# Context projections as three bf16 products, a split completion signal for the stacked keys, and a new item order in two cross attentions

## The reference

```python
kh = (memory @ wk.T + bk).reshape(Bx, -1, H, d).transpose(0, 2, 1, 3)
vh = (memory @ wv.T + bv).reshape(Bx, -1, H, d).transpose(0, 2, 1, 3)
a = softmax(einsum('bhnd,bhmd->bhnm', qh, kh) / sqrt(d))
ca = einsum('bhnm,bhmd->bhnd', a, vh)
```

## Time and profile before

| | |
|---|---|
| median of 3 runs | 2066.61 us (2065.41 to 2078.53) |
| profiled execution, its own time | 2067.55 us |
| its span, first to last instruction | 2065.7 us |
| mean granted clock of TensorE | 0.95 of full speed |
| busy: PE, DVE, ACT, POOL | 1846.1, 1401.8, 1259.3, 325.4 us |
| XA0, main loop | about 89 to 590 us |
| XA1, main loop | about 1039 to 1765 us |

### The profile page before, as it was taken

How to read it: one execution, slowest core, us unless ns; L and a number is a source line. 1 busy time by engine, 2 the same in 40 slices (tenths; PEclk the granted TensorE clock), 3 DMA queues, 4 the chain that set the end, 5 groups by cost and what they waited for, 6 DMA issues and landing times. The chain is left out here.

```text
span 2065.7 us, 65669 instructions
## 1 busy us (share of the span) xinstructions
PE 1846.1 (89%) x28558; PEld 1189.3 (58%) x28576; DVE 1401.8 (68%) x2411; ACT 1259.3 (61%) x1785; POOL 325.4 (16%) x331
## 2 busy tenths in 40 slices
PE   8899999999989577999689999999999999757798
PEld 5577777777765364444355656656566665425443
DVE  3677777777753665566487888888888888238465
ACT  3477777777744371333267877777777877438343
POOL 4000000000030430111001100010001100014265
PEclk8999999999999787999799999999999999878999
DMA  4454555445400300555644455455555452030011
GB/s 146 103 142 126 130 133 136 128 125 131 112 10 1 62 4 16 148 146 144 121 87 98 83 93 92 84 97 88 93 88 94 85 93 40 1 63 4 22 41 42
DMA packets 66540, 178.18 MB, mean 86 GB/s; under 512 B 20276, under 2 KB 24500, under 8 KB 65844
## 3 DMA queue, kind: packets, MB, share of 16 engines
q1 hardware_dynamic: 64436, 170.85, 37.7%
q10 hardware_dynamic: 1824, 3.20, 0.7%
HBM read 84.39 MB, written 1.31 MB: 41 GB/s over the span
## 5 line engine op out<-in xcount | busy, mean ns | idle before, releaser
L604 ACT ACTIVATE Pb<-ps 128x1024 f32<-128x1024 f32 (+2 forms) x640 | 633.7, 1001 | 206.5 <-PE ps L553 158.8
L676 DVE TENSOR_REDUCE MX<-ps 128x2 f32<-128x804 f32 (+1 forms) x386 | 368.9, 986 | 59.8 <-PE ps L520 58.7
L573 PE MATMUL ps<-Pb,V 128*17 128x64 f32 (+1 forms) x13312 | 360.3, 248 | 9.7 <-issue 4.9
L678 DVE TENSOR_REDUCE MX<-ps 128x1 f32<-128x402 f32 (+1 forms) x512 | 278.1, 571 | 102.2 <-PE ps L524 92.9
L573 PEld LDWEIGHTS ps<-Pb,V 128*17 128x17 f32 (+1 forms) x13312 | 256.3, 97 | 97.0 <-issue 64.3
L520 PE MATMUL ps<-KST,QW 50*128 50x402 bf16 (+1 forms) x1024 | 176.6, 340 | 23.9 <-ACT V L623 17.1
L553 PE MATMUL ps<-QW,KST 50*128 50x128 bf16 (+1 forms) x3328 | 165.5, 219 | 29.9 <-ACT Pb L604 29.3
L504 PE MATMUL ps<-W,CT 128*128 128x128 f32 (+1 forms) x1144 | 168.3, 286 | 1.1 <-ACT V L623 1.1
L553 PEld LDWEIGHTS ps<-QW,KST 50*128 50x128 bf16 (+1 forms) x3328 | 101.1, 96 | 113.1 <-ACT Pb L604 83.9
L496 PE MATMUL ps<-CT,W 128*128 128x402 f32 (+1 forms) x352 | 146.8, 542 | 18.0 <-DMA CT<-ctxT 12.1
L524 PE MATMUL ps<-KST,QW 96*128 96x402 bf16 (+1 forms) x512 | 154.3, 339 | 4.3 <-issue 2.2
(11 more groups left out here) (235 smaller groups left out, 2764.8 us busy)
## 6 DMA issues: line engine op xcount, KB each, us to landing
CT<-ctxT SPq DMA_DIRECT2D x44, 800.5 KB, 4.8
KST<-HL SPq DMA_DIRECT2D x320, 100.1 KB, 3.0
KST<-C SPq DMA_DIRECT2D x320, 100.1 KB, 3.0
Pb<-routed SPq DMA_DIRECT2D x64, 256.0 KB, 3.9
ABO<-ctxT SPq DMA_DIRECT2D x10, 800.5 KB, 5.4
T<-ctxT SPq DMA_DIRECT2D x10, 800.5 KB, 4.4
KST<-HL SPq DMA_DIRECT2D x128, 50.0 KB, 2.7
KST<-C SPq DMA_DIRECT2D x128, 50.0 KB, 2.7
```

The source lines that it names most:

```text
L573: mm = nc.tensor.matmul(ps[32 * quad:32 * quad + m, SUM, oc:oc + nh * S], V[0:n, b % 2, tile, v0:v0 + m], Pb[0:n, buffer(b, x), ti * att.W ...
L604: nc.scalar.activation(Pb[0:n, buffer(b, x), 0:banks * 512].rearrange("p (a c) -> p a c", a=banks), score_banks(b, x)[0:n, 0:banks, :], AC ...
L676: nc.vector.reduce_max(MX[:, b % 2, 2 * j:2 * j + 2], work(job)[:, :, 0:n], AX.X).then_inc(freed["dve"], 1)
L678: nc.vector.reduce_max(MX[:, b % 2, j:j + 1], work(job)[:, 0:n], AX.X).then_inc(freed["dve"], 1)
```

## The change

1. Both projections of the context become three bf16 products: high weights by high context, low weights by high context, high weights by low context. The high context is a stepped view of the float32 context. POOL computes the low context (one 128x1601 subtraction per item) into new buffers. The weights are split once per attention, the high part by two ACT copies and the low part by two POOL subtractions. K of item 0 stays float32.
2. K waits for POOL's low context (semaphore `cross_low`) instead of the context's DMA; V of item 0 waits for the low weights as well. POOL has the subtraction for item b+3 as the first thing of turn b, ahead of the queries for item b+2.
3. The stacking DMAs run group by group, and raise one semaphore for groups 0 and 1 and another for groups 2 and 3. M0 waits for the first, M8 for the second.
4. Both orders are rewritten. K and H stand at the head of a turn. M0 stands behind S0 in XA0, and still first in XA1. In XA1, P-1 moves from ahead of S0 to behind M1.

```diff
-    16: ("M0 K0 K1 H0 H1 P-1 S0 M1 K2 K3 S1 H2 H3 V0 M2 S2 V1 M3 S3 M4 P0 M5 S4 P1 M6 S5 M7 P2 M8 S6 M9 P3 P4 S7 "
-         "M10 P5 M11 S8 M12 P6 P7 M13 S9 V2 M14 S10 M15 P8 P9 S11 V3 P10 R0 P11 S12 "),
-    8: ("P-1 M0 M1 K0 K1 K2 H0 K3 V0 H1 H2 H3 M2 S0 M3 V1 M4 S1 M5 S2 M6 M7 M8 P0 P1 M9 S3 M10 M11 S4 M12 V2 M13 "
-         "S5 M14 S6 V3 M15 P2 P3 P4 R0 P5 ")}
+    16: ("M0 K0 H0 K1 H1 S0 M1 P-1 K2 H2 K3 H3 S1 V0 M2 S2 V1 M3 S3 M4 P0 M5 S4 M6 P1 M7 S5 P2 P3 M8 S6 M9 P4 P5 S7 "
+         "M10 M11 P6 S8 M12 P7 M13 S9 V2 M14 S10 M15 P8 P9 S11 P10 V3 R0 S12 P11 "),
+    8: ("K0 K1 P-1 H0 K2 H1 H2 K3 V0 H3 S0 M0 M1 V1 M2 M3 S1 S2 M4 M5 M6 P0 P1 M7 M8 S3 M9 S4 M10 P2 M11 M12 V2 M13 "
+        "S5 M14 S6 M15 V3 P3 P4 P5 R0 ")}
...
+        def split_weights(role, eng, att, call):
...
+                if role == "act":
+                    nc.scalar.activation(hi, full, ACT.Copy).then_inc(hi_s, 1)
+                if role == "pool":
+                    eng.wait_ge(hi_s, 2 * call + k + 1)
+                    nc.gpsimd.tensor_tensor(lo, full, hi, ALU.subtract).then_inc(lo_s, 1)
...
+            def context_hi(b):
+
+                return context(b).bitcast(BF16).rearrange("p (n t) -> p n t", t=2)[:, :, 1]
...
                 if j == 0:
-                    eng.wait_ge(*context_in(b))
+                    eng.wait_ge(*(lowered(b) if b else context_in(b)))
                 banks_free(job)
-                nc.tensor.matmul(work(job)[:, 0:n], w(f"{t}_k"), context(b)[:, c0:c0 + n],
-                                 start=True, stop=True).then_inc(filled, 1)
+                if b:
+                    for i, (wp, moving) in enumerate(((0, context_hi(b)), (1, context_hi(b)), (0, context_lo(b)))):
+                        mm = nc.tensor.matmul(work(job)[:, 0:n], WS[:, 0, wp, :], moving[:, c0:c0 + n],
+                                              start=(i == 0), stop=(i == 2))
...
-                    mm = nc.tensor.matmul(heads_out(work(job)[0:n, i * D:(i + 1) * D]), context(b)[:, k0:k0 + n],
-                                          heads(w(f"{t}_v")), start=True, stop=True)
+                    for k, (still, wp) in enumerate(((context_hi(b), 0), (context_hi(b), 1), (context_lo(b), 0))):
+                        mm = nc.tensor.matmul(work(job)[0:n, i * D:(i + 1) * D], still[:, k0:k0 + n],
+                                              WS[:, 1, wp, :], start=(k == 0), stop=(k == 2))
...
-                    eng.wait_ge(*kst_landed(b))
+                if j in (0, 8):
+                    eng.wait_ge(*kst_landed(b, j // 8))
...
+            def pool_context_low(b):
+
+                eng.wait_ge(*context_in(b))
+                nc.gpsimd.tensor_tensor(context_lo(b), context(b), context_hi(b), ALU.subtract
+                                        ).then_inc(sem("cross_low"), 1)
...
+                pool_context_low(0)
+                pool_context_low(1)
                 eng.wait_ge(vones, 2 * past + 2)
                 eng.wait_ge(*inputs_ready)
                 pool_queries(0)
                 pool_queries(1)
+                pool_context_low(2)
                 for b in range(B):
+                    if b + 3 < B:
+                        pool_context_low(b + 3)
                     for kind, j in att.order:
                         if kind == "M" and j == 0 and b + 2 < B:
                             pool_queries(b + 2)
```

More of the change, by code:

```diff
@@ L221, in bass_perceiver_kernel @@
         CT = sb("CT", [128, 2, NK], F32)
+        CL = sb("CL", [128, NK], BF16)
+        WS = sb("WS", [128, 2, 2, D], BF16)
         KST = sb("KST", [128, 3, 4, NK], BF16)
@@ L418, in project_split @@
             return lo_s, n + 1
+        def split_weights(role, eng, att, call):
+            hi_s, lo_s = sem("weights_hi"), sem("weights_lo")
+            if role == "pool":
+                eng.wait_ge(sem("ones_set"), 2 + call)
+            values = w(f"{att.name}_v").rearrange("p (h e) -> p h e", e=att.d + 1)[:, :, 0:att.d]
+            for k, full in enumerate((w(f"{att.name}_k").rearrange("p (h e) -> p h e", e=att.d), values)):
+                hi, lo = [WS[:, k, part, :].rearrange("p (h e) -> p h e", e=att.d) for part in range(2)]
+                if role == "act":
+                    nc.scalar.activation(hi, full, ACT.Copy).then_inc(hi_s, 1)
+                if role == "pool":
+                    eng.wait_ge(hi_s, 2 * call + k + 1)
+                    nc.gpsimd.tensor_tensor(lo, full, hi, ALU.subtract).then_inc(lo_s, 1)
         def load_context(role, eng, att, item):
@@ L431, in cross_attention @@
             s_ctx = [sem(f"cross_ctx{i}") for i in range(3)]
-            s_kst = [sem(f"{t}_kst{i}") for i in range(3)]
+            s_kst = [[sem(f"{t}_kst{i}_groups{p}") for p in range(2)] for i in range(3)]
             freed = {"act": sem("cross_freed_act"), "dve": sem("cross_freed_dve")}
@@ L444, in cross_attention @@
             half = [slice(64 * h, 64 * h + HALF) for h in range(2)]
-            def heads(x):
-                return x.rearrange("p (h e) -> p h e", e=att.d + 1)[:, :, 0:att.d]
             def keys(b):
@@ L493, in pe_keys @@
                 if j == 0:
-                    eng.wait_ge(*context_in(b))
+                    eng.wait_ge(*(lowered(b) if b else context_in(b)))
                 banks_free(job)
-                nc.tensor.matmul(work(job)[:, 0:n], w(f"{t}_k"), context(b)[:, c0:c0 + n],
-                                 start=True, stop=True).then_inc(filled, 1)
+                if b:
+                    for i, (wp, moving) in enumerate(((0, context_hi(b)), (1, context_hi(b)), (0, context_lo(b)))):
+                        mm = nc.tensor.matmul(work(job)[:, 0:n], WS[:, 0, wp, :], moving[:, c0:c0 + n],
+                                              start=(i == 0), stop=(i == 2))
+                else:
+                    mm = nc.tensor.matmul(work(job)[:, 0:n], w(f"{t}_k"), context(b)[:, c0:c0 + n], start=True, stop=True)
+                mm.then_inc(filled, 1)
             def pe_values(b, j):
                 job = (b, "V", j)
+                if b == 0 and j == 0:
+                    eng.wait_ge(sem("weights_lo"), 2 * past + 2)
+                    eng.wait_ge(*lowered(0))
                 banks_free(job)
@@ L610, in act_keys @@
                 if j == 0 and b >= 2:
-                    eng.wait_ge(*kst_landed(b - 2))
+                    for p in range(2):
+                        eng.wait_ge(*kst_landed(b - 2, p))
                 eng.wait_ge(*filled_with(job))
@@ L727, in sp_stack @@
                     eng.wait_ge(scores, units + (b - 2) * NE)
-                if att.halved:
-                    for g in range(4):
+                for g in range(4):
+                    landed = s_kst[b % 3][g // 2]
+                    if att.halved:
                         for h in range(2):
                             a, c0 = 64 * h, 32 * g + 16 * h
[L732 to L736, removed]
+                            eng.dma_start(KST[a:a + 32, b % 3, g, :], keys(b)[c0:c0 + 16, :, 0:NK]).then_inc(landed, 16)
+                            eng.dma_start(KST[a + 34:a + 50, b % 3, g, :], keys(b)[c0:c0 + 16, 0, 0:NK]).then_inc(landed, 16)
+                    else:
+                        for p, term in enumerate((0, 1, 0)):
                             eng.dma_start(KST[32 * p:32 * p + 32, b % 3, g, :], keys(b)[32 * g:32 * g + 32, term, 0:NK]
-                                          ).then_inc(s_kst[b % 3], 16)
+                                          ).then_inc(landed, 16)
             if part == "first":
@@ L1844, in program @@
             eng.wait_ge(rest_w, 32)
+            split_weights(role, eng, XA0, 0)
             q_lo = project_split(role, eng, 0, w("c_wq"), "bq0", s, HLQ)
@@ L1898, in program @@
             load_context(role, eng, XA1, 1)
+            split_weights(role, eng, XA1, 1)
             keys_out = cross_attention(role, eng, XA1, "first", "bo1")
```

14 lines of the change are left out of this document (9 added, 5 removed).

## The result

The changed kernel takes 1990.32 us (median of four runs, 1988.54 to 1998.57), against 2068.78 us for the kernel before (2065.41 to 2078.53, four runs; the table ahead of the prediction has three of them). The ratio is 0.9621, with a 95% interval from 0.9578 to 0.9664. The forecast was 2016, with 1996 to 2050: the sign was right, and a gain of 78 us stands where 52 were expected, outside the range.

A forecast was written before the change was run, and what follows sets the result against it. XA0 was taken as bound by PE's queue, XA1 by ACT's work plus bare gaps. From 2067.55 us, 42 and 0.9 (XA0) and 10.5 (XA1) off, 0.6 added (split weights): 2014.8, rounded up to 2016; range 1996 to 2050.

The forecast's parts named there:

- the 1.58 us step: XA1: exponential (1.02 us) and wait for its score job (0.56) repeat every 1.58 us, unless ACT evicts in the gap.
- 18.6 us of ACT's work: XA1: ACT works 18.6 us of a 23.28 us turn; with 4.8 us of waits that is the whole turn.
- What can shrink is ACT's stretch from exponential 11 to exponential 1: XA1, turn boundary: of 6.89 us, exponential 1 starts about 0.3 us sooner by the new order; 0.35 taken.
- they need the exponential's end, not a faster K or V: XA1, exponentials from S3 to S12: their gaps stay as they are, no gain from the cheaper projections.
- The bound of 22.5 us for XA1: XA1 turn: 18.6 us of ACT's work plus seven gaps of 0.56 without an eviction, 0.75 less than now.
- rival B: XA1 gets all of its bound, 22 us instead of 10, with the same XA0: 2004 us, down to 1995; chance 0.08.
- the order in XA0: XA0, new order laid out by hand: waits leave a 14.6 us turn, so 1.4 of PE's 1.7 us is kept.
- slack on POOL: POOL's low-context subtraction and query build finish early enough: over 3 us of slack in a 14.6 us turn.
- A: V gets no cheaper, or DVE and the three banks pace XA0 at 15.3 us a turn: 2040 us; chance 0.13.
- C: XA1 loses 0.5 us a turn by a late output copy and K2, XA0 keeps 0.7: 2061 us; 0.12 with E.
- D: POOL's subtraction blocks DVE, adding 0.7 to 2.2 us a turn in XA1, 0.8 in XA0: some 2130 us; chance 0.05.
- E: TensorE's clock falls in XA1 as PE works less, giving back some 1.5 us a turn: 2060 us; 0.12 with C.

The follow-up runs named there:

- k_only: The changed kernel with V's projection back in float32 and K's in bf16; 2021.7 us, ratio 0.975.
- v_only: The changed kernel with K's projection back in float32 and V's in bf16; 2034.8 us, ratio 0.980.
- orders_only: The kernel before with both new orders, everything else as before (float32 projections, one signal); 2059.7 us, ratio 0.993.
- p_ahead: The changed kernel with P-1, and the output copy behind it, back ahead of S0 in XA1; 1997.34 us.
- again: The changed kernel once more, unaltered, with a second profile; 1991.64 us, ratio 0.960.
- one_signal: The changed kernel with M0 waiting for both halves of the stacking DMAs; 1992.78 us.
- pool_twice: The changed kernel with every low context computed twice on POOL, one after the other; 1994.24 us.
- two_products: The changed kernel without the product of low weights with high context, in K and V; 1978.41 us, ratio 0.954.

## Why the prediction was wrong

**What bounds the kernel: right for XA0, half right for XA1.** PE's queue paces XA0: k_only and v_only add up. In XA1 the 1.58 us step is there in every kernel. But "18.6 us of ACT's work" was taken for a fixed quantity.

**The step that failed: "What can shrink is ACT's stretch from exponential 11 to exponential 1", sized at about 0.3 us and given to the order, with nothing for K's cheaper matmuls.** The stretch shrank by 0.65 (6.90 to 6.25), and k_only against orders_only (6.25 against 7.00) gives it to K's price alone. The order moved time inside the stretch and removed none: 7.00 with orders_only, 6.26 with the old orders and bf16, 6.37 in p_ahead. The prediction saw the 0.36 us wait before exponential 12 go (the step fell by 0.33) and had about 0.2 us of waiting for K0 right (0.24). It left out that two float32 K jobs, 1.55 us of PE, already held up ACT's evictions and the score job behind them, twice a turn. In the trace of before that is hard to see: no idle time is printed, only pairs of evictions of 1.21 and 1.26 us, where the changed kernel has 1.08 and 1.13. Each single eviction is 0.60 us long in both; what differs is when the second begins, 0.62 and 0.66 us after the first before, 0.49 and 0.54 in "again". The same failure is in "they need the exponential's end, not a faster K or V": the steps to 4 and 11 lost 0.10 and 0.11 with V in bf16.

**The bound of 22.5 us for XA1 was no bound.** It added busy time (18.6) and seven bare gaps (3.9). The 18.6 was read off a window of 50 us, which is 2.15 turns; over 29 whole turns it is 18.30, and the same sum gives 22.2, below the 22.29 that was measured. Nor was it fixed: it fell to 17.65 as such waits inside the pairs went. The lower end of the range was made with this bound (rival B), so the range missed the result.

**In the sum:** XA1 was given 10.5 us; it gave 27.1 from item 0 to item 31 in "again". This is 17 of the 26 us missing. The rest is from the start of the program (last section) and small terms: "again" lost 3.6 us ahead of XA0's first shift and 2.0 behind XA1, where the prediction had +0.6 and nothing. The 3.6 is luck of the clock there, and not a gain of the change.

**XA0: 1.4 predicted, 1.45 measured** (1.39 in "again"), 43 us of the sum against 42.9. That the total came out so close is partly luck, as its parts didn't: 1.7 us of PE work was to come off and 0.3 to be lost to waits. Measured, the bf16 jobs gave 1.14 and the order 0.25 (or 0.90 and 0.5, in the other sequence). The K part was worth 0.5 (0.65 to 1.05 expected), V 0.67 (0.8 to 0.9), and "the order in XA0" was costed as a loss where it was a gain.

**Nothing for the split signal, 2.86 us for POOL, slack on POOL:** right (one_signal; the group's 2860 ns; pool_twice). The stepped view costs nothing: right.

**The rivals.** A fell on its first reason (0.055 us in a V job). Its second reason, banks and DVE in XA0, begins to be true in two_products. B named the side on which the result came, but its reason was another: the 0.93 us wait before exponential 11 is 0.82 in "again", and the bulk of the gain is at the K evictions. C's mechanism was real, 0.45 us at the step to 1 in orders_only, and was paid back at the steps to 12 (0.33) and 9 (0.09). D and E didn't come: DVE's durations and the clock of 1.00 in XA1 are unchanged.

## What to carry to other kernels

When an engine's instructions stand close together, compare their starts before calling the engine full. Here two evictions of 0.60 us, with the second one's input ready in time, began 0.49 to 0.54 us apart; a pair that begins 0.62 to 0.66 us apart is waiting for its producer, though no idle time is printed. A matmul job that stands in PE's queue ahead of a serially bound job can be on the critical path, through its own eviction or through the job behind it; price it by all that it holds up. And a lower bound made by adding busy time and waits is only as good as the busy time is fixed: take it over whole turns, and ask what waits it hides.

## What the runs showed of the hardware

TensorE's clock at the start of the program differs between executions of one kernel, and the start takes 3 to 6 us longer when it is low. The window from 20 to 30 us, first in the changed kernel's first profile, then in "again":

```profile
20.00:30.00 10.00, 10.00 (x48) 9.93 (x47) 3.11 (x6) 1.12 (x3) 3.70 (x1) 0.50 0.24 57
```

```profile
20.00:30.00 10.00, 10.00 (x55) 7.03 (x55) 5.23 (x10) 2.59 (x5) 3.70 (x1) 1.00 0.24 55
```

The same program had a granted clock of 0.50 there in one and 1.00 in the other, and the query projection began at 65.73 us in one and 59.57 in the other. All profiles fall into these two kinds: 1.00 and a projection at 59.5 to 61.2 us in five, 0.50 to 0.61 and 64.1 to 65.9 in the nine others, the kernel before among them (0.61, 64.07). About 4.5 us of the difference between its profile and "again" (64.07 less 59.57) are from this, and not from the change. What sets the clock there stays open. Nor does it explain all of the spread: executions of the kernel before lie between 2063 and 2084 us.

In "again", the V jobs' weight loads took a median of 98 ns both from the stepped view (tile `T`) and from the contiguous low context (tile `CL`). Their matmuls, twelve in a row and accumulated by threes, took 0.055 us each, as the contiguous score matmuls (0.056) did.
